# First attention: several masked heads of a bank in one product and one maximum; the halves' maximum from one operand

## What is computed

```python
q = q.reshape(bs, seq_len, NUM_HEADS, HEAD_DIM).transpose(0, 2, 1, 3)    # 32 heads of 16
k = k.reshape(bs, seq_len, NUM_KV_HEADS, HEAD_DIM).transpose(0, 2, 1, 3) # 8
q = apply_rope(q, 0)
k = apply_rope(k, 0)
scores = jnp.einsum('bhqd,bhkd->bhqk', q, k) / math.sqrt(HEAD_DIM)
causal = jnp.tril(jnp.ones((seq_len, seq_len), dtype=bool))
scores = jnp.where(causal[None, None, :, :], scores, jnp.float32(-1e+20))
attn = jax.nn.softmax(scores, axis=-1)
out = jnp.einsum('bhqk,bhkd->bhqd', attn, v)
```

## Time and profile before

| | |
|---|---|
| median of 3 runs | 1275.75 us (1274.57 to 1278.98) |
| profiled execution | 1276.31 us, span 1274.6 us |
| mean granted clock of TensorE | 0.94 |
| busy share of the span: PE, DVE, ACT, POOL | 93%, 73%, 51%, 29% |

### The profile page before, as it was taken

The page is one execution under the profiler, slowest core; times in us unless marked ns, Lnnn a source line. Parts: engine busy times, 40 slices in busy tenths (PEclk is TensorE's granted clock), DMA queues, the critical chain, the costliest instruction groups (busy, mean ns, idle before and its releaser), DMA issues.

```text
span 1274.6 us, 21543 instructions
## 1 busy us (share of the span) xinstructions
PE 1179.1 (93%) x6800; PEld 743.4 (58%) x6800; DVE 928.0 (73%) x2974; ACT 655.5 (51%) x1007; POOL 375.6 (29%) x505
## 2 busy tenths in 40 slices
PE   4998999999889998999989899999997999989888
PEld 1875343444358997545878644444432889855478
DVE  5789878999527878662768799899991578676365
ACT  1721556666555644444546026666666465445542
POOL 1431232222145520214624314111223455002261
PEclk9997679999899999899999958999999999989999
DMA  9465411121001013200250752112200100430001
GB/s 315 145 165 108 134 26 27 27 73 56 2 1 52 2 34 92 68 2 1 71 180 24 200 133 77 27 27 60 69 3 1 52 2 1 100 93 2 1 10 58
DMA packets 40309, 80.39 MB, mean 63 GB/s; under 512 B 6060, under 2 KB 7596, under 8 KB 40060
## 3 DMA queue, kind: packets, MB, share of 16 engines
q1 hardware_dynamic: 40200, 79.02, 21.8%
HBM read 48.98 MB, written 27.08 MB: 60 GB/s over the span
## 4 chain that ended last, share of the span: by engine, by line
PE 72%; DVE 14%; issue 5%; ACT 3%; DMA 3%; POOL 2%; SPq 1%; DVEq 0%; ACTq 0%; POOLq 0%
PE bank L1029 16%; PE bank L897 12%; PE bank L804 7%; PE bank L805 6%; PE bank L806 6%; DVE maxes L1247 5%; PE bank L1011 5%; DVE unused L1243 4%; PE bank L790 3%; PE bank L1005 3%; PE bank L907 2%; PE bank L829 2%; PE bank L831 2%; PE bank L830 2%; PE bank L879 1%
## 5 line engine op out<-in xcount | busy, mean ns | idle before, releaser
L1478 ACT ACTIVATE probs<-bank 128x1024 f32<-128x1024 f32 (+3 forms) x416 | 365.5, 911 | 308.1 <-PE bank L1011 225.6
L897 PE MATMUL bank<-ops 48*128 48x512 f32 (+3 forms) x960 | 318.0, 432 | 14.0 <-DVE maxes L1243 3.9
L1243 DVE CUSTOM_DVE_ANT_0 unused<-bank,causal 128x128 bf16<-128x128 f32 (+3 forms) x640 | 278.5, 485 | 46.5 <-PE bank L897 43.1
L1590 POOL TENSOR_SCALAR_AFFINE_SELECT probs<-probs 128x256 f32<-128x256 f32 (+1 forms) x256 | 118.9, 465 | 597.4 <-ACT probs L1478 596.4
L897 PEld LDWEIGHTS bank<-ops 48*128 48x128 f32 (+1 forms) x960 | 162.1, 204 | 194.8 <-DVE maxes L1243 81.3
L1029 PE MATMUL bank<-probs,v_mem 128*17 128x512 f32 (+6 forms) x1920 | 248.9, 526 | 2.1 <-ACT heads_raw L1465 1.5
L1247 DVE TENSOR_REDUCE maxes<-bank 128x1 f32<-128x512 f32 x320 | 206.8, 684 | 42.2 <-PE bank L897 41.4
L1011 PE MATMUL bank<-ops 50*128 50x512 f32 (+2 forms) x640 | 179.5, 455 | 4.4 <-ACT probs L1478 4.3
L1011 PEld LDWEIGHTS bank<-ops 50*128 50x128 f32 x640 | 88.8, 201 | 59.3 <-ACT probs L1478 30.5
L804 PE MATMUL bank<-ops,xT 128*128 128x512 f32 (+1 forms) x288 | 113.8, 395 | 5.7 <-DVE xT L1088 2.6
L1088 DVE TENSOR_TENSOR xT<-bank,xT 128x512 fp32r<-128x512 f32 (+1 forms) x96 | 61.5, 643 | 73.4 <-ACT xT L1357 73.2
(11 more groups left out here) (119 smaller groups left out, 1887.0 us busy)
## 6 DMA issues: line engine op xcount, KB each, us to landing
query_rows_dram<-ops SPq DMA_DIRECT2D x48, 256.0 KB, 3.8
ops<-query_rows_dram SPq DMA_DIRECT2D x64, 192.0 KB, 4.3
w_odd<-staging_wqkv SPq DMA_DIRECT2D x4, 1536.0 KB, 6.5
x<-x_dram SPq DMA_DIRECT2D x16, 256.0 KB, 5.6
ops<-features SPq DMA_DIRECT2D x64, 64.0 KB, 2.0
ops<-ops SPq DMA_DIRECT2D x16, 256.0 KB, 3.1
out_dram<-x SPq DMA_DIRECT2D x16, 256.0 KB, 2.0
staging_wqkv<-wqkv_dram SPq DMA_DIRECT2D x2, 1536.0 KB, 16.1
```

Of the source, the lines that this page charges most:

```text
L897: last = mm(dst[:, h * w:(h + 1) * w], queries(a, u)[rows, t // 4, hi, t % 4 * P:(t % 4 + 1) * P], keys(a, u, hi)[rows, HALF * kp:HALF * k ...
L1243: V.tensor_tensor_reduce(unused[:, masked % 3, 0:w], part, causal[:, HALF - w:], 1.0, NEG, ALU.add, ALU.max, dst).then_inc(s["max_done"].s ...
L1478: A.activation(probs[:, e % 6, :, 0:cols], scores[:, 2 * (e % 2):2 * (e % 2) + 2, 0:cols], ACT.Exp, scale=a.scale).then_inc(s["exp"].sem, 1)
L1590: G.affine_select(out=p, in_=p, compare_op=ALU.is_ge, fill=0.0, base=0, pattern=pattern, channel_multiplier=-1).then_inc(s["masked"].sem, 1)
```

## The change

Banks with two masked heads of the first attention are masked on PE: a product of an identity in bf16 (`identb`, new, filled by POOL at the start) with `causal`, repeated for each head, opens the accumulation, and the score products of the heads are added to it. DVE then takes the maxima of both heads with one reduction. Other banks stay as they were. In `shift_parts`, for both attentions, the maximum over the two halves is a reduction over one operand with the halves as its last axis, and goes to a free place of `maxes`.

```diff
+    def product_mask(self, bank):
+
+        return self.row_tiles == 2 and bank[4] and len(bank[3]) > 1
...
-        ops = [m[4] for m in self.max_banks for _ in m[3]]
+        ops = [m[4] and not self.product_mask(m) for m in self.max_banks for _ in m[3]]
...
+        identb = sb("identb", [P, P], BF16)
...
-            pe.wait_ge(s_const.sem, 6)
+            pe.wait_ge(s_const.sem, 7)
...
                     operands_ready(b, st, u, t)
+                    together, m = a.product_mask(a.max_banks[n]), len(heads_in)
+                    if together:
+                        mm(dst[:, 0:m * w].rearrange("p (h k) -> p h k", h=m), identb[:, :],
+                           causal[:, HALF - w:].unsqueeze(1).to_broadcast([P, m, w]), start=True, stop=False)
                     for h, (r, hi) in enumerate(heads_in):
                         rows = a.score_rows(r, a.part_rows)
                         last = mm(dst[:, h * w:(h + 1) * w], queries(a, u)[rows, t // 4, hi, t % 4 * P:(t % 4 + 1) * P],
-                                  keys(a, u, hi)[rows, HALF * kp:HALF * kp + w], start=True, stop=True)
+                                  keys(a, u, hi)[rows, HALF * kp:HALF * kp + w], start=not together,
+                                  stop=not together or h == m - 1)
...
+                    together = a.product_mask(a.max_banks[n])
+                    if together:
+                        h0, m = a.heads.index(heads_in[0]), len(heads_in)
+                        V.tensor_reduce(maxes[:, u % 2, kp, h0:h0 + m, t:t + 1], src[:, 0:m * w].rearrange("p (h k) -> p h k", h=m),
+                                        AX.X, ALU.max).then_inc(s["max_done"].sem, m)
+                    for h, head in enumerate(heads_in if not together else ()):
...
-                    V.tensor_tensor(mx, mx, maxes[:, u % 2, 1, 0:nh, 4:8], ALU.max).then_inc(s["shift_step"].sem, 1)
+                    both = maxes[:, u % 2, :, 0:nh, 4:8].rearrange("p k h t -> p h t k")
+                    mx = maxes[:, u % 2, 1, 0:nh, 0:4]
+                    V.tensor_reduce(mx.unsqueeze(3), both, AX.X, ALU.max).then_inc(s["shift_step"].sem, 1)
...
+            mask_tile(identb, 0.0, ALU.not_equal, 1.0, 2).then_inc(s_const.sem, 1)
             G.memset(causal[:, :], 0.0).then_inc(s_pool.sem, 1)
-            pool.wait_ge(s_pool.sem, 2)
+            pool.wait_ge(s_pool.sem, 3)
```

More of the change, by code:

```diff
@@ L1232, in ring_read @@
                     t, kp, w, heads_in, diag = a.max_banks[n]
-                    masked = u * len(a.masked_ops) + sum(len(m[3]) for m in a.max_banks[:n] if m[4])
-                    for h, head in enumerate(heads_in):
+                    masked = u * len(a.masked_ops) + sum(len(m[3]) for m in a.max_banks[:n] if m[4] and not a.product_mask(m))
+                    together = a.product_mask(a.max_banks[n])
[4 more added lines that the diff above has]
+                    for h, head in enumerate(heads_in if not together else ()):
                         dst = maxes[:, u % 2, kp, a.heads.index(head), t:t + 1]
@@ L1505, in _ @@
                    allow_small_or_imprecise_dtypes=True).then_inc(s_const.sem, 1)
-            pool.wait_ge(s_const.sem, 6)
+            pool.wait_ge(s_const.sem, 7)
             def split_chunk(b, st, k):
```

## The result

The changed kernel takes 1306.88 us, the median of four runs (1305.85 to 1312.77), against 1275.16 us for the kernel before beside it. The ratio is 1.0258 with a 95% interval of 1.0213 to 1.0303: slower by 2.6%. Its profiled execution has a span of 1304.1 us, that of before 1274.6.

What follows compares the result with a forecast made beforehand. PE and DVE, both nearly full in the first attention's units, were taken to hold each other. 1.9 us a unit (1.3 and 0.6) over 14 units added 27 us to 1275.75: 1302.5 us, own range 1295 to 1313.

Steps and rivals of the forecast that it cites:

- The bound: First attention's 28.24 us unit: PE (27.46 us) and DVE (26.29 us) hold each other, neither with over 8% to give.
- DVE's terms: First attention: common reductions save DVE 0.7 us a unit, the maximum over the halves about 0.2 us.
- The halves' 0.2 us: Maximum over the halves: POOL's wait mostly moves one instruction on, winning about 0.2 us a unit, ends 0 and 0.48.
- PE's terms: Eight mask products: drains, weights not loaded ahead and streamed columns add 3.6 us of PE a unit.
- The identity's weights: Mask product on PE: loading the bf16 identity was taken to cost 0.06 us, bounds 0 and 0.10 us.
- The walk: Through one unit's order: 1.3 us late at tiles 0 and 1, 0.6 us at tiles 4 and 5, together 1.9 us.
- the prediction's own lower end: Units of the first attention: 1.4 us a unit if the identity's loads cost 0, the range starting at 1295 us.
- Unit 0: Its masks fall into the product chain and the run-up, where PE waits anyway: 0, give or take 1 us.
- That DVE sets the unit (1): First attention: PE swallows the masks, each of 16 units loses 0.9 to 1.2 us, 1257 to 1262 us; chance 0.13.
- That the mask only streams (2): Mask on PE: no drain, no load, 0.11 or 0.22 us a bank, 1275 to 1279 us; chance 0.12.
- The clock (3): Added matmuls keep PE at 2.4 GHz, 10 to 20 us come back, 1282 to 1293 us; chance 0.10.
- That nothing is absorbed (4): PE's waits stay and most of the 3.6 us comes on top: 42 to 55 us, 1318 to 1331; chance 0.08.

Runs made afterwards that it cites:

- e3: Changed kernel without the mask's products, the eight two-head banks left unmasked, common reductions kept: 1272.87 us, ratio 0.9965.
- e9: Kernel before with the two turns of the shift in a unit moved to just in front of the values: 1270.78 us, ratio 0.9948.
- e1: Kernel before with only the maximum over the halves made one reduction over one operand: 1274.92 us, ratio 0.999.
- e2: Changed kernel with the maximum over the halves from two operands again, so the masks' product alone: 1311.32 us, ratio 1.0248.
- e8: Kernel before with a 128-row, 32-column product, overwritten by the scores, ahead of each of the eight banks: 1302.83 us, ratio 1.0193.
- e5: Changed kernel with each of the eight mask products made twice in a row, the second accumulating: 1328.58 us, ratio 1.0395.
- e6: Changed kernel with product and common reduction for tiles 0 and 1 only, tiles 4 and 5 as before: 1307.42 us, ratio 1.0229.
- e7: Changed kernel with product and common reduction for tiles 4 and 5 only: 1285.67 us, ratio 1.0082.
- e4: Changed kernel with the mask's product over 64 rows instead of 128, half of the mask left out: 1273.62 us, ratio 0.9979.

## Why the prediction was right, and where it wasn't

**The bound.** The prediction read two engines that hold each other, each with under 8% to give. The runs make PE the stronger of the two: 0.87 us less work on DVE shortened the unit by 0.13 (e3), two changes of kind less on PE by 0.25 with DVE's work as it was (e9). The low idle time of DVE in the earlier trace rows was no sign that its work set the pace.

**DVE's terms.** All held in size. Behind the reduction of a bank with 256 values the next operation starts 0.34 us later, for a predicted 0.33, in the timeline of DVE at tile 4 (after):

```profile
301.11 0.43 DVE L1247 TENSOR_REDUCE maxes<-bank 128x2 f32<-128x256 f32 x1 [0.42 <-PE bank L906]
301.69 0.43 DVE L1247 TENSOR_REDUCE maxes<-bank 128x2 f32<-128x256 f32 x1 [0.15 <-PE bank L906]
302.03 2.47 DVE L1262 TENSOR_REDUCE maxes<-bank 128x1 f32<-128x512 f32 x4
...
306.87 0.69 DVE L1262 TENSOR_REDUCE maxes<-bank 128x1 f32<-128x512 f32 x1 [0.30 <-PE bank L906]
```

(301.69 to 302.03; the 0.58 us before that hold a wait.) The halves' 0.2 us, with the hold moved to the next instruction, is what the timelines of e1 and e2 show.

**PE's terms.** The drain of 0.10 us and the score weights of 0.10 us behind it stand in the timeline as predicted. The Trainium skill (TensorEngine Tiling (Array Packing), Key Properties) says that changing the tiling mode drains TensorE, without a size; the trace agrees, at 0.10 us a change. The identity's weights were mis-sized: I took 0.06 us from a 128x128 load of another type, and 0 is what shows. Ahead of the product of 289.28 there is the drain and nothing more, and its record of 0.39 us is as long as that of any 512 columns in the earlier trace rows. The Trainium skill (TensorE: Matmul & The Clock Gate, Weight-path perf modes), by which such a load takes about half as long as one in fp32, was nearer to it than my row. The trace agrees: the records of the identity's loads take 0.10 us (median 96 ns), those of 128x128 loads in fp32 0.19, and nothing of the 0.10 stands on the path.

One change that the prediction counted doesn't exist. It charged the second bank of tile 1, behind the turn of the shift, with a change of kind; PE after shows none, 0.12 us from start to start:

```profile
290.03 0.29 PE L912 MATMUL bank<-identf,shifts 128*32 128x128 f32 x1
290.16 0.38 PE L902 MATMUL bank<-causal,identb 128*128 128x512 bf16 x1
```

So this bank pays 0.22 us, its columns, and not 0.38; with the loads at 0 the masks bring 3.0 us of PE a unit, and not 3.6. Behind values the change is there, as counted. The changes alone, 8 x 0.10 + 5 x 0.20 = 1.8 us of PE by the prediction's terms, cost 1.10 a unit (e8); the columns, 1.28, cost 1.08 (e5).

**The walk.** At tiles 0 and 1 it was nearly right in each step. From the halves' maximum to the values were 0.31 us before and 288.08 - 286.97 = 1.11 after: 0.80 us late, for 0.84 predicted. DVE idles 1.52 us (1.65). Tile 2's second masked operation starts at 292.36, 5.39 us behind the halves' maximum, where the earlier trace rows have 282.65 - 278.55 = 4.10: 1.29 us late (1.33), and e6 gives 1.30 for the two tiles alone. At tiles 4 and 5 it was short: DVE's reduction at 306.87 starts 6.52 us behind PE's first work for tile 4 (300.35), where the earlier trace rows have 268.19 - 262.39 = 5.80. That is 0.72 us late, for 0.6, and e7 gives 0.73. PE there, after:

```profile
300.35 0.28 PE L902 MATMUL bank<-causal,identb 128*128 128x256 bf16 x1
300.57 0.43 PE L906 MATMUL bank<-ops 48*128 48x128 f32 x2
300.93 0.28 PE L902 MATMUL bank<-causal,identb 128*128 128x256 bf16 x1
301.15 0.32 PE L906 MATMUL bank<-ops 48*128 48x128 f32 x1
```

The four scores that went in together in the earlier trace rows are two pairs now, 0.58 us apart. The 0.12 us that the walk lacked are the whole unit's error: 2.03 against 1.9. It is smaller than it had a right to be. With the identity's load at the 0 that it has, the prediction's own lower end, 1.4 us a unit, would have come out, and the 0.6 us between that and 2.03 come from what the walk left out in other places: about 0.1 by the values of tile 0, 0.1 more by tile 2 and 0.4 at tiles 4 and 5 (the three delays above, less the walk's without 0.06 for each load). Two errors met, so the closeness of 1.9 to 2.03 is in part luck. What the second is made of was only placed, not divided further.

**Unit 0 and the outside.** "0, give or take 1 us" for the masks of the first unit was wrong: the first maximum comes 3.2 us later, with the clock at 1.2 GHz from 113 us on before and from 114 us on after. The run-up had less cover than I gave it. With 2.3 and 1.9 us elsewhere, which are within what these stretches vary by, 7.4 us lie outside the fourteen units, for which the sum had nothing.

**The rivals.** That DVE sets the unit (1) falls with e3: DVE's saving became idle time. That the mask only streams (2) falls with e8, 1.10 us a unit without columns; the 64-row product of e4 is this rival made real, and gives its result, no change (0.9979). The clock (3) gave back 6.3 us between the two profiled executions where the rival needed 10 to 20, and e1 shows that as much comes and goes without any added matmul. That nothing is absorbed (4) falls with the unit: 3.0 us of PE went in by the terms as measured, and with DVE's 0.13 added back 2.16 came out. The forecast put 27 us on top of before; the medians differ by 31.7 and the spans by 29.5. By the spans that is 14 x 2.03 = 28.4 in place of 27, less 6.3 for the clock, plus 7.4 outside the units: the mechanism was right, and of these three differences only the unit's and the run-up's 3.2 us are clear of what the profiles vary by.

## What to carry to other kernels

Cost an added matmul by its neighbours, not by its columns: one of another kind than those around it (here 128 rows among 48) pays for two changes of kind and for the weights behind them, while one of the same kind can run beside the other half's (1.28 us of columns cost 0.34 us instead of 2.16 here). Where two engines are both nearly full, test which one sets the pace by taking a little off each; idle time alone doesn't say. And look for changes of kind that are already there: moving the two turns of the shift in a unit right ahead of the values gained 0.5% with no work removed.

## What the runs showed of the hardware

- A change between 64-row and 128-row matmuls costs 0.10 us of drain whatever the columns are: 0.12 us from a product of 32 columns to the next scores (162.08 to 162.20), 0.21 from one of 256, 0.32 from one of 512.
- Not only the rows make the kind: behind the turn of a shift a 128x128 product starts after 0.12 us, the values, which use 128 rows and 17 columns of weights, after 0.21 us, the drain in it.
- Weights of 128 columns in bf16 behind such a change show no time of their own, while score weights of 48 rows lengthen the pair behind it from 0.40 to 0.50 us.
- POOL's hold falls on the TENSOR_TENSOR and the TENSOR_SCALAR, 0.65 and 0.43 us, and not on the TENSOR_REDUCE over the same tile, 0.19 us; it lasts until POOL's operation ends.
- More matmul work on PE does not settle what clock is granted: the kernel with products in four banks ran 3.4 us at 1.2 GHz in nearly every unit of its first sequence, the one with eight ran all units but the first of each sequence at 2.4 GHz.
